# Attention of a fused block on one NeuronCore: where the softmax sums are divided out, and on which engine the rotary products are added

## The reference

```
y  = x @ Wc^T + b + scale[id] * ((x @ A[id]^T) @ B[id]^T)      # condition, low rank by adapter
x1 = x + attn1(y)                                              # 32 heads of 16, causal, rotary
h  = attn2(x1)                                                 # 32 heads of 128, 8 key/value heads
out = x1 + ffn(h)                                              # 512x512 and a gated low-rank part
attn2: q, k, v = x1 @ Wq^T, x1 @ Wk^T, x1 @ Wv^T
       q, k = rotate(rmsnorm(q) * w, pos), rotate(rmsnorm(k) * w, pos)
       keys, values = 512 cached (16 pages of 32, by a table) + 128 new
       o = softmax(q keys^T / sqrt(128), masked by length) values
       h = o (128 x 4096) @ Wo^T
```

## Time and profile before

| | |
|---|---|
| median of 3 runs | 1234.5 us (1233.25 to 1235.74) |
| the profiled execution: its own time | 1234.96 us |
| the profiled execution: span from first to last instruction | 1233.2 us |
| granted TensorE clock, mean | 0.991 of full speed |
| busy: TensorE / weight loads | 1183.4 us (96%) / 996.0 us (81%) |
| busy: VectorE / ScalarE / GpSimd | 988.6 (80%) / 845.0 (69%) / 964.4 us (78%) |

### The profile page before, as it was taken

One profiled execution on the slowest core, in us unless ns is written; L12 is line 12 of the kernel. 1 busy time (PEld: TensorE's weight loads), 2 busy tenths in 40 slices (PEclk: granted clock), 3 DMA queues, 4 the chain that ended last, 5 costly groups with the idle time before them and its releaser, 6 DMA issues.

```text
span 1233.2 us, 23998 instructions
## 1 busy us (share of the span) xinstructions
PE 1183.4 (96%) x6872; PEld 996.0 (81%) x6872; DVE 988.6 (80%) x2396; ACT 845.0 (69%) x2441; POOL 964.4 (78%) x715
## 2 busy tenths in 40 slices
PE   6899998789999999999999999999999999999998
PEld 4577775578888888888888888888888888888778
DVE  3577866478988888888888888888898889888876
ACT  2777777476777676767777777677677777676731
POOL 1656656478888888979897989798889888888852
PEclk9999998999999999999999999999999999999999
DMA  8556555256566666666666566656665665666651
GB/s 264 211 194 243 215 219 181 75 121 149 135 138 153 156 141 142 161 156 139 152 152 149 129 149 153 156 131 158 154 155 136 156 148 133 139 154 151 137 154 69
DMA packets 336037, 191.33 MB, mean 155 GB/s; under 512 B 149153, under 2 KB 320162, under 8 KB 334882
## 3 DMA queue, kind: packets, MB, share of 16 engines
q1 hardware_dynamic: 334896, 189.63, 60.5%
q10 hardware_dynamic: 1010, 0.17, 0.1%
HBM read 101.66 MB, written 37.75 MB: 113 GB/s over the span
## 4 chain that ended last, share of the span: by engine, by line
PE 76%; POOL 12%; ACT 5%; issue 4%; DVE 2%; DMA 1%; SPq 1%; DVEq 0%; ACTq 0%; POOLq 0%
PE ps L1300 15%; PE ps L1301 15%; PE ps L1302 15%; PE ps L1368 4%; PE ps L1361 4%; PE ps L1360 4%; POOL b_p_l L1748 4%; POOL b_w_l L1706 3%; PE ps L254 3%; PE ps L266 2%; PE ps L316 2%; PE ps L1328 2%; POOL b_w_l L1712 1%; PE ps L306 1%; PE ps L332 1%
## 5 line engine op out<-in xcount | busy, mean ns | idle before, releaser
L1748 POOL TENSOR_TENSOR b_p_l<-b_moved,b_p_h 128x1280 fp32r<-128x1280 f32 x128 | 380.0, 2969 | 20.0 <-ACT b_p_h L1505 20.0
L1499 ACT ACTIVATE b_sm<-b_sm,b_mn 128x640 f32<-128x640 f32 x256 | 212.9, 832 | 120.0 <-DVE b_mn L1605 112.4
L1605 DVE CUSTOM_DVE_ANT_0 b_sm<-ps,mask_row,b_rstd 128x640 f32<-128x640 f32 x256 | 222.3, 868 | 65.1 <-PE ps L1302 65.0
L1634 DVE SCALAR_TENSOR_TENSOR b_hacc<-ps,b_ri,b_hacc 128x512 f32<-128x512 f32 x248 | 184.5, 744 | 10.5 <-PE ps L1302 4.5
L1300 PE MATMUL ps<-b_w_h,x1t_h 128*128 128x512 f32 (+1 forms) x512 | 180.0, 352 | 5.0 <-POOL b_w_l L1712 4.5
L1301 PE MATMUL ps<-b_w_l,x1t_h 128*128 128x512 f32 (+1 forms) x512 | 173.5, 339 | 0.0
L1302 PE MATMUL ps<-b_w_h,x1t_l 128*128 128x512 f32 (+1 forms) x512 | 173.1, 338 | 0.0
L1505 ACT ACTIVATE b_p_h<-b_moved 128x1280 fp32r<-128x1280 f32 x128 | 163.0, 1273 | 10.9 <-DMA b_moved<-b_blk_first 7.7
L1300 PE MATMUL ps<-b_kt_h,b_qt_h 128*128 128x320 f32 x512 | 163.9, 320 | 0.9 <-DVE b_mn L1605 0.9
L1302 PE MATMUL ps<-b_kt_h,b_qt_l 128*128 128x320 f32 x512 | 158.4, 309 | 0.0
L1301 PE MATMUL ps<-b_kt_l,b_qt_h 128*128 128x320 f32 x512 | 158.2, 309 | 0.0
(11 more groups left out here) (176 smaller groups left out, 3156.6 us busy)
## 6 DMA issues: line engine op xcount, KB each, us to landing
b_moved<-b_blk_first SPq DMA_DIRECT2D x256, 160.0 KB, 3.2
b_moved<-b_blk_second SPq DMA_DIRECT2D x256, 160.0 KB, 3.1
kv_of_batch<-in_kv SPq DMA_DIRECT2D x128, 256.0 KB
b_ck<-kv_of_batch SPq DMA_DIRECT2D x64, 256.0 KB, 4.2
b_cv<-kv_of_batch SPq DMA_DIRECT2D x256, 64.0 KB, 2.5
raw<-in_w SPq DMA_DIRECT2D x32, 384.0 KB, 4.8
raw<-in_wo SPq DMA_DIRECT2D x32, 256.0 KB, 4.2
a_xt<-in_xt SPq DMA_DIRECT2D x8, 256.0 KB, 7.2
```

Of the source, the lines that this page charges most:

```text
L1499: act.activation(sm[:, h % 2], sm[:, h % 2], ACT.Exp, bias=mn[:, m.b % 2, h:h + 1], scale=-1.0, accum_out=rs[:, m.b % 2, h:h + 1]).then_in ...
L1605: dve.tensor_tensor_reduce(sm[:, h % 2], score_row(h), mask_row[:, m.b], rstd[:, m.b % 4, h:h + 1], -MASKED, ALU.add, ALU.min, mn[:, m.b % ...
L1634: dve.scalar_tensor_tensor(out=hacc[:, m.b], in0=ps[:, OUT[h], :], scalar=share, in1=hacc[:, m.b], op0=ALU.mult, op1=ALU.add).then_inc(h_s ...
L1748: pool.tensor_tensor(pair_of(p_l, pair), moved_pair(pair), pair_of(p_h, pair), ALU.subtract).then_inc(ml_sb, 1)
```

## The change

The reciprocals (`ri`, 128 queries x 4 heads) are sent to DRAM (`send_shares`) and read back as one row of 512 numbers into every partition of `share_rows` (`spread_shares`). VectorE's new `normalize` multiplies the attention output in PSUM by that row, in place, reading the row with a step of four words. Then ScalarE takes the high part and VectorE the low part as before. All four heads' projections now go into one PSUM bank (`SM`) as one accumulation of 12 matmuls, the eight with `o_h` first, and `accumulate` is one addition for an item. VectorE does the rotary sums: `rope_products` writes the sine product into bank `SM` and the new key's into a free part of bank `PJK`, and the sums read it from there (items 0 and 1 keep the old way). All 12 matmuls of an item stand together behind `scores(one, 0)`. `invert` moves into the item's own slot, `turned_key` ahead of the weights and `exponent(m, 2)` on ScalarE, VectorE's chunk of wq to the end of its slot. In `phase3`, `most` and `lowt` are put into tiles that have come free, so `load_small` waits for the cached keys.

```diff
@@ SyncE
+            def send_shares(m):
+                sp.wait_ge(ri_sb, m.n + 1)
+                sp.dma_start(share_dram[m.b % 2], ri[:, m.b % 2]).then_inc(shares_out, 16)
+            def spread_shares(m):
+                sp.wait_ge(shares_out, 16 * (m.n + 1))
+                wait(sp, on_ps, m.n)
+                row = share_dram[m.b % 2].rearrange("q h -> (q h)").unsqueeze(0).broadcast_to([P, P * REP])
+                sp.dma_start(share_rows[:], row).then_inc(shares_in, 16)
             def slot(m, one, two, last):
+                if last:
+                    spread_shares(last)
                 blocks_across(m, 0)
                 blocks_across(m, 1)
+                send_shares(m)
...
             slots(sp, slot)
+            spread_shares(end)
             load_small(sp)
@@ TensorE
             def values_of_highs(m):
-                wait(pe, h_sb, REP * m.n - 1)
+                wait(pe, ol_sb, m.n)
...
+            def out(m):
+                if m.ahead(3).exists():
+                    pe.wait_ge(qr_sb, m.n + 4 - EARLY)
+                pe.wait_ge(oh_sb, m.n + 1)
+                wait(pe, h_sb, m.n)
+                tiles = [slice(h * P, (h + 1) * P) for h in range(REP)]
+                for h in range(REP):
+                    if m.b == 0:
+                        pe.wait_ge(wol_sb, KT * m.g + h + 1)
+                    pe.matmul(ps[:, SM, :], o_h[:, tiles[h]], wo_h[:, h], start=h == 0, stop=False)
+                    pe.matmul(ps[:, SM, :], o_h[:, tiles[h]], wo_l[:, h], start=False, stop=False)
+                pe.wait_ge(ol_sb, m.n + 1)
+                for h in range(REP):
+                    mm = pe.matmul(ps[:, SM, :], o_l[:, tiles[h]], wo_h[:, h], start=False, stop=h == REP - 1)
+                mm.then_inc(wo_ps, 1)
@@ ScalarE
             def output(m):
-                act.wait_ge(pv_ps, m.n + 1)
-                wait(act, wo_ps, REP * m.n)
+                act.wait_ge(on_ps, m.n + 1)
+                wait(act, wo_ps, m.n)
@@ VectorE
             def rope_products(m):
...
+                turned = halves(rb[:], REP) if m.n < EARLY else ps[:, SM, :].rearrange("p (h t d) -> p h t d", h=REP, t=2)
+                dve.tensor_tensor(turned, swapped(q, REP), sines, ALU.mult)
+                dve.tensor_tensor(ra[:], q.rearrange("p (h d) -> p h d", h=REP), over(cw[:, m.b, 0], REP), ALU.mult).then_inc(qab_sb, 1)
+            def rope_queries(m):
+                dve.wait_ge(qab_sb, m.n + 1)
+                dve.tensor_tensor(ra[:], ps[:, SM, :].rearrange("p (h d) -> p h d", h=REP), ra[:], ALU.add).then_inc(qr_sb, 1)
             def new_values(m):
...
+                dve.tensor_tensor(rest..., turned, sw..., ALU.mult)
+                dve.tensor_tensor(ka[:], k, cw[:, m.b, 1], ALU.mult).then_inc(kab_sb, 1)
+                dve.wait_ge(kab_sb, m.n + 1)
+                dve.tensor_tensor(kb[:], rest, ka[:], ALU.add).then_inc(kab2_sb, 1)
+            def normalize(m):
+                dve.wait_ge(pv_ps, m.n + 1)
+                dve.wait_ge(shares_in, 16 * (m.n + 1))
+                hold(dve)
+                o = ps[:, OT, :].rearrange("p (h q) -> p h q", h=REP)
+                dve.tensor_tensor(o, o, share_rows[:].rearrange("p (q h) -> p h q", h=REP), ALU.mult).then_inc(on_ps, 1)
+            def accumulate(m):
+                dve.wait_ge(wo_ps, m.n + 1)
+                if m.g == 0:
+                    dve.tensor_copy(hacc[:, m.b], ps[:, SM, :]).then_inc(h_sb, 1)
+                    return
+                dve.tensor_tensor(hacc[:, m.b], ps[:, SM, :], hacc[:, m.b], ALU.add).then_inc(h_sb, 1)
```

More of the change, by code:

```diff
@@ L1413, in slot @@
                 if last:
-                    out(last, 0)
-                    out(last, 1)
+                    out(last)
                 if m.n == end.n - 1:
@@ L1429, in _ @@
             low_rows(pe, 0)
-            for h in range(REP):
-                out(end, h)
+            out(end)
             batches(pe)
@@ L1526, in slot @@
                     cache_keys(one)
+                    turned_key(one)
                 if m.b == 1:
@@ L1649, in slot @@
                 minima(m, 2)
-                turn_blocks(m, 1)
                 if one:
                     queries(one)
+                turn_blocks(m, 1)
                 if before:
-                    accumulate(before, 3)
+                    accumulate(before)
                 if m.n == end.n:
@@ L1659, in slot, with q_weights, kv_weights @@
                 turn_blocks(m, 3)
+                invert(m)
                 if one:
                     new_keys(one)
+                if two:
+                    rope_products(two)
+                if last:
+                    normalize(last)
+                if two:
+                    rope_queries(two)
+                if last:
+                    output(last)
                 if m.n == end.n - 1:
                     h_rest(dve, 0)
-                if two:
-                    rope_products(two)
-                if m.b == 5:
-                    low_weights(m.g + 1, 1)
-                if last:
-                    output(last)
-                    invert(last)
                 if one:
                     minima(one, 0)
-                if last:
-                    accumulate(last, 0)
-            def low_weights(g, c):
+                if m.b == 5:
+                    q_weights(m.g + 1, 1)
+            def q_weights(g, c):
                 dve.wait_ge(wqh_sb, KT * g + c + 1)
                 dve.tensor_tensor(w_l[:, c, 0:D], raw[:, c, 0:D], w_h[:, c, 0:D], ALU.subtract).then_inc(wql_sb, 1)
-            def low_kv_weights(g):
+            def kv_weights(g):
                 dve.wait_ge(wkvh_sb, g + 1)
@@ L1685, in low_kv_weights, with out_weights @@
                 dve.tensor_tensor(w_l[:, :, cols], raw[:, :, cols], w_h[:, :, cols], ALU.subtract).then_inc(wkvl_sb, 1)
-            vector_first(dve, (rope_products, new_values, queries, new_keys, minima, low_weights, low_kv_weights))
+            def out_weights(g, c):
+                dve.wait_ge(woh_sb, KT * g + c + 1)
+                dve.tensor_tensor(wo_l[:, c], raw[:, c, 0:D], wo_h[:, c], ALU.subtract).then_inc(wol_sb, 1)
+            vector_first(dve, (rope_products, new_values, queries, new_keys, minima, q_weights, kv_weights))
             slots(dve, slot)
-            accumulate(end.before(), 1)
-            accumulate(end.before(), 2)
-            accumulate(end.before(), 3)
+            accumulate(end.before())
             choose(dve, 0)
             h_rest(dve, 2)
-            invert(end)
+            normalize(end)
             output(end)
-            for h in range(REP):
-                accumulate(end, h)
+            accumulate(end)
             rows_dve(dve)
@@ L1752, in slot @@
                     rms(one)
-                    key_sum(one)
                 if last:
@@ L1776, in _ @@
             pool.wait_ge(const_sb, 1)
-            gpsimd_first(pool, (q_weights, kv_weights, rope_queries, rms, key_sum, cache_keys, cache_values))
+            gpsimd_first(pool, (q_weights, kv_weights, rope_queries, rms, cache_keys, cache_values))
             slots(pool, slot)
```

103 lines of the change are left out of this document (33 added, 70 removed).

## The result

The changed kernel takes 1239.42 us (median of 13 runs, 1236.54 to 1245.43) against 1234.27 for the kernel before on the same chip: ratio 1.0043, 95% interval 1.0031 to 1.0054. It is slower by 0.43%, where the prediction said 1228.0 and most probably faster: outside the forecast's own 1222 to 1232, inside the wide range of 1221 to 1246, and on the other side of no change. The profiled execution took 1239.51 us, span 1237.7, so 4.5 us more span than before (1233.2).

The account below looks back on a forecast made before the run. TensorE's matmuls were taken to bound the middle. Groups -0.95 us each, -7.1 over 60 slots, start -1, end +1.5: -6.6, so 1228.4 us profiled, 1228.0 median; own range 1222 to 1232, 8 in 10 for 1221 to 1246.

Parts of the forecast that it names:

- Together -1.6 us a group: Middle slots: lighter GpSimd ends TensorE's waits for wk's and wv's low part and the new key, 1.6 us a group.
- I take 0.69: VectorE's normalize, reading SBUF with a step of four words: 0.69 us, taken from new_keys, which reads PSUM so.
- TensorE bounds the middle: Middle 60 slots: a slot lasts as long as its matmuls, TensorE busy 879.27 of 884.29 us; 12 matmuls an item stay.
- First loop: TensorE and minima: scores(m, 3) waits for minima(m, 1), its load 0.11 late; costs 0.05 us a slot, bounds 0 and 0.12.
- GpSimd's relief removes the stops: Middle: without rope_queries (1.36 us a slot) and key_sum on GpSimd, TensorE's waits go, -1.6 us a group.
- Late next is the copy by ScalarE: Middle, at kv_weights: it starts about 0.9 us sooner, then limited by ScalarE's copy, which is not sooner than before.
- Second loop: VectorE through normalize and o_h to out and the next minima(m, 1): 14.2 us, about 0.35 left, doesn't bind.
- The rule set aside: VectorE's strided SBUF read: full rate needs two adjacent words, so normalize an estimated 1.04 to 1.44 us; kernel near 1252.
- Rival 1: Second loop: normalize's strided read binds, a group +0.6, 1239.5 us, slower; decides from 0.4 us more; chance 0.27.
- Rival 2: VectorE's chunk of wq is caught behind GpSimd's low_probs: up to 2.9 us a group, 1238; chance 0.06.
- Rival 3: Waits only move: kv_weights late by ScalarE, x1 loads by 3.5 us, first loop 0.12 a slot: 1234; chance 0.17.
- SyncE and the end: FFN loads wait for the last shares, +3.5 us; slots 62 and 63 give about 2 back: net +1.5, bounds -0.5 and +4.
- The start, -1: Kernel start: key_sum and an exponential leave the chain, -1 us, bounds -2 and 0.

Follow-up runs that it names:

- e1: Changed kernel with normalize's loop order swapped, shares read word after word and the 128-word step on PSUM: 1232.45 us, ratio 0.9985 to the kernel before.
- e2: Changed kernel with out in two parts, the four low matmuls moved behind scores(1) of the next slot: 1233.44 us, ratio 0.9995 to the kernel before.
- e4: Changed kernel with all four ScalarE copies of wq ahead of o_h in b = 5: 1231.67 us, ratio 0.9978 to the kernel before.
- f3: Changed kernel plus an unused VectorE copy of the shares ahead of normalize, from the fourth item: 1266.57 us, ratio 1.0268 to the kernel before.
- f2: Kernel of e8 with the shares read in steps of four words again: 1226.61 us, ratio 0.9939 to the kernel before.
- e3: Changed kernel with the FFN's small loads issued ahead of the last item's spreading of shares: 1238.28 us, ratio 1.0028 to the kernel before.
- e5: Changed kernel without the division and its share transfers, normalize multiplying by ones: 1235.64 us, ratio 1.001 to the kernel before.
- e8: Kernel of e6 with the next item's cached values issued ahead of the chunks of wo in b = 0: 1222.90 us, ratio 0.9912 to the kernel before.
- e6: Changed kernel with the edits of e1 to e4 together: 1224.85 us, ratio 0.9918 to the kernel before.

## Why the prediction was wrong

It failed at two steps: "Together -1.6 us a group", the stops that GpSimd's relief was to remove, and "I take 0.69" for `normalize`. The second alone turns the sign (e1), but without it the change would still have missed the forecast. By its own steps, against the profile:

- **TensorE bounds the middle**: right. Clock 1.00, TensorE busy 881.85 of 886.80 us, the same matmuls.
- **First loop, 0.05 us a slot** (0 to 0.12): right, in the mechanism too: the load comes 0.11 late as worked out (the rows at 663.39), a quiet slot grows by 0.065 and e2 takes it away; 3.9 us instead of 3.0.
- **GpSimd's relief removes the stops**: wrong but for b = 0, where `turn_new`'s wait went and nothing took its place. Over the 60 slots, stops beyond quiet slots were 884.29 - 60 x 14.54 = 11.9 us before and are 886.80 - 60 x 14.605 = 10.5 after, where 0.25 x 7.5 = 1.9 were forecast. 8.6 of the 9.6 us by which the middle was missed (+2.5 against -7.1) lie here. Of the 10.5, 8 x 0.24 + 7 x 0.29 + 7 x 0.69 = 8.8 stand in b = 1, 5 and 6, 1.0 more in the two long slots, most of the rest in the first two slots. Of the 8.6, 3.95 are the long `normalize` at work in b = 1 and b = 5 (e1); 7 x 0.65 = 4.6 are the stop of b = 6, which e1 leaves and e4 takes away. The text looked only at what stood ahead of `kv_weights` on GpSimd in b = 6 and said "Late next is the copy by ScalarE"; it did not follow that chain back through b = 5, where four copies, `o_h` and three GpSimd subtractions pass the lateness on. It had the fact (in b = 5 "ScalarE's `o_h` and all behind it come 0.95 later") and priced it at 0.15 us.
- **`normalize` at 0.69**: 1.07. The row it was taken from read PSUM with a step of four words, and the step was in SBUF here. e1 prices the mistake at 7.0 us (in the profiles 4.3 in the middle, 2.1 at the end, 1.1 at the start, where single executions differ by more). With 0.70 the change gives -1.8 us against before, still not -6.
- **Second loop 14.2 us, slack 0.35**: good. f3 puts it at 14.50 with the longer `normalize`, so 14.12 without. It closes through the queries' sum, though, which the text had ending "at the time of `o_h`" and did not follow further. Quiet slots were not bound by it, and the places said to have the least cover (b = 1, b = 5) are those that stopped.
- **The rule set aside**: the Trainium skill, Vector Engine (DVE) Microarchitecture Reference, section 5.2, lost to the nearest row. Its lower figure, an estimated 1.04 us, was right (1.07 measured), its upper one, a slot of 14.95 us, was not reached. The weighing took a row of another memory over a rule on this one.
- **Rival 1** came nearest: 1239.5 forecast for it, 1239.42 measured, at 0.38 us where it said "decides from 0.4". But by other terms: it had +4.5 in the middle and +0.5 for start and end; measured are +2.5 and +2.0, and the stops of b = 5 and 6 reach TensorE through ScalarE and GpSimd, not through `o_h`. (Its price at half rate, 0.55 us, comes to 0.59 by its own numbers, 512 x 0.44 / 384; nothing hangs on it.)
- **Rival 2**, the caught chunk: not in this kernel (1.00 us, 6 times), but real, as e4 and f2 show.
- **Rival 3**, the waits only move, had the mechanism of b = 6: "`kv_weights` is late by ScalarE". With the short `normalize` this is the picture, and its 1234 stands near e1's 1232.45. It got 0.17.
- **SyncE and the end**: the wait for the shares was right (3.1 us), its worth less (e3: about 1). The 2 us expected back from slots 62 and 63 did not come. `normalize` is on their path, but that is 0.33 us a slot; even in e1 these two take only 0.7 us less than before, and what holds them is not shown. Net +2.2 for +1.5.
- **The start, -1**: -0.2 in this trace, less than single executions differ there; not tested.

What stays open: what makes single slots of b = 1 long (15.59, 15.09). SyncE's issue of one chunk took 2.67 us ahead of the longer one (but others of up to 3.13 us cost nothing), e5 clears the share transfers, and e8's reordering is not told apart from e6.

## What to carry to other kernels

Work taken off an engine is worth something only on the chain that is late: follow the wait back through every engine and the slot before, and look where the freed time turns into waiting for something else. A new instruction on a loop with little slack should be priced in the very memory and step it uses; if the nearest row is of another memory, let the range and the likeliest case follow the rule that speaks of this one. Here two edits of a few lines did most of it: the loop order swapped so that the step falls on PSUM (e1), and copies that were ready put ahead of a wait instead of behind it (e4). Each alone made the change slightly faster than the kernel before, and with e2 and e3 they turned +0.4% into -0.8%.

## What was unexpected of the hardware

- VectorE, 128x512 float32 product, one operand in PSUM: 1.07 us with a step of four words on the SBUF operand (after); 0.70 with that operand word after word and a step of 128 words, four at a time, on the PSUM operand and the PSUM output (e1).
- Writing PSUM from VectorE took about what SBUF does (after: 0.70 against 0.65 to 0.69).
- A VectorE subtraction with two SBUF inputs took 0.69 us when it began 0.04 us ahead of GpSimd's and 3.39 when it began 0.12 us behind it (e4). A plain SBUF copy is hit as well: 0.43 alone, up to 1.03 beside GpSimd (f3).
